# Grouped convolution and per-sample mix: the fp32r parts of x taken straight from the loaded tile, without a tile between

## The chip, the cores and the metric

The kernel runs on one core of a Trainium2 chip. The metric is the device time of one execution in microseconds (us), the median over several runs; smaller is better.

## The reference

The input x has 64 samples of 128 channels by 2048 positions, in fp32. Two residual blocks follow each other:

```python
# L0: grouped convolution along the positions, 4 groups of 32 channels, 9 taps, plus a context per sample
x = x + conv(x, weight, groups=4, padding=4) + (cond @ c_weight.T)[:, :, None] + bias[None, :, None]
# L1: a 128 x 128 matrix per sample, a softmax mixture of 8 matrices
h = gelu(gelu(cond @ W0 + b0) @ W1 + b1)
att = softmax(h @ W2 + b2)
agg_w = einsum('bk,koi->boi', att, weight[..., 0]);  agg_b = att @ bias_k
x = x + einsum('boi,bih->boh', agg_w, x) + agg_b[:, :, None]
```

## The kernel before, in words

The sum is kept near fp32 precision with TensorE's fp32r format: each operand is split into a rounded part (`_hi`) and what the rounding left (`_lo`), and a product is made of three matmuls, hi by hi, hi by lo and lo by hi.

**Phases.** The 2048 positions of a sample are split into PH = 4 phases, position 4n + q being column n of phase q. The convolution of one group of 32 channels is then M = 12 shifted products, 3 matmuls each, so CONV = 36 matmuls of 32 rows by 512 columns. The mix is MIX = 12 matmuls for each phase r. The four groups t run on the four row quarters of TensorE at once, group t LAG = 4 steps behind group t - 1. A slot is the time of one sample: 48 steps of four matmuls. At steps 0 to 35 group 0 convolves sample s, at steps 36 to 47 it mixes sample s - 1; the other groups do the same 4, 8 and 12 steps later.

**Per sample.** SyncE loads x into `x_in` (1 MB, two buffers). ScalarE copies `x_in` to `x_ph`, reading every fourth element (a step of 16 bytes) and writing the four phases one after the other (`split_phases`, L418). VectorE rounds `x_ph` to `x_hi` (`round_x`, a cast, L480) and takes `x_lo` = `x_ph` - `x_hi` (`rest_x`, L486). TensorE convolves into the PSUM tile `y_ps` (L357). ScalarE rounds y to `y_hi` (`round_y`, L428, one for each group), VectorE takes `y_lo` (`rest_y`, L497). GpSimd builds the mix matrix of the sample in `mix_prod`, `mix_sum_f`, `mix_f`, `mix_parts` (`mix_matrix`, L588 to L611); SyncE stores it to DRAM (`store_mix`, L235) and loads it back four times into `mix_rep` (`load_mix`, L247). TensorE mixes (L377), ScalarE takes the sum with the bias to `z_out` (`take_z`, L439, two halves), SyncE stores it (L255).

**Order.** Every engine has its own list, written out by hand. In slot s, SyncE does load_mix(s), store_mix(s + 1), store(s - 2), load(s + AHEAD), with AHEAD = 4; ScalarE does take_z(s - 2) twice, split_phases(s + 2), round_y(s, 0..3); VectorE does round_x(s + 1), rest_x(s + 1), rest_y(s, 0..3). An engine waits at the head of its list, and what stands behind waits too. `x_hi` has two buffers, so that of sample s + 1 can be written when the convolution of sample s - 1 has ended, which is when slot s begins. There is one `y_ps`: group g of the next sample can start when `y_lo` of group g has been taken.

**Start.** VectorE makes the convolution weights (`cw_rep` L501 by a read with a step of 36 bytes, `wt_f`, `wt_lo`, then `cw_lo` L513), then x_hi and x_lo of sample 0. In slot 0 TensorE carries, between its steps, the small matrix products of the softmax, and VectorE the element-wise work of it: att_diag (L541), `rest_x((0, 1))`, then after TensorE's L339 `table` (L545 to L557), on which GpSimd's first mix matrix waits. Samples are counted from 0.

Of the kernel before, what the change touches and what calls it, by code (L numbers as in the profile page):

```python
# [13 lines left out]
U = 4  # L14
Q = 32
DMA = 16
AHEAD = 4
LAG = 4


# [32 lines left out]
def cond_resid_kernel(nc, x, cond, bias, conv_w, ctx_w, w0, b0, w1, b1, w2, b2, mix_w, mix_b, out):  # L53
# [13 lines left out]
    with ExitStack() as stack:  # L67
# [7 lines left out]
            return [make(f"{name}{k}", *args) for k in range(2)]  # L75

        x_in = two(sb, "x_in", [P, T])
        x_ph = two(sb, "x_ph", [P, PH, N])
        x_hi = two(sb, "x_hi", [P, PH, N + 2], F32R)
        x_lo = two(sb, "x_lo", [P, PH, N + 2], F32R)  # L80

# [86 lines left out]
        table_made = sem("table_made")  # L168

        x_loaded = two(sem, "x_loaded")  # L170
        x_split_ph = sem("x_split_ph")

        x_hi_made = sem("x_hi_made")
        x_lo_made = sem("x_lo_made")
# [34 lines left out]
        @block.sync  # L209
        def _(sp):  # L210
            def ahead(*values):

                for v in values:
                    if not isinstance(v, int):
                        sp.compute_val(v)
                return values

            def load(s):
                if not exists(s):
                    return  # L220
                b, taken = ahead(number(s), done(s, lag=-2))

                at_least(sp, x_split_ph, taken)
                sp.dma_start(x_in[buf(s)][:, :], x[b, :, :]).then_inc(x_loaded[buf(s)], DMA)

            def store_mix(s):

                if not exists(s):
                    return
                b = buf(s)  # L230
                made, taken = ahead(done(s), DMA * G * uses(s))
                sp.wait_ge(mix_made, made)

                at_least(sp, mix_loaded[b], taken)
                sp.dma_start(mix_dram[b][:, :, :], mix_parts[b][:, :, :].bitcast(F32)).then_inc(mix_stored[b], DMA)  # L235

            def load_mix(s):

                if not exists(s):
                    return  # L240
                b = buf(s)
                stored, mixed = ahead(DMA * (uses(s) + 1), done(s, PH, lag=-2))
                sp.wait_ge(mix_stored[b], stored)

                at_least(sp, z_ready, mixed)
                for r in range(PH):
                    sp.dma_start(mix_rep[b][Q * r:Q * r + Q, :, :, :].bitcast(F32).rearrange("c g h o -> c g (h o)"),  # L247
                                 mix_dram[b].rearrange("(g c) h o -> c g (h o)", g=G)).then_inc(mix_loaded[b], DMA)

            def store(s):  # L250
                if not exists(s):
                    return
                b, read = ahead(number(s), done(s, 2))
                sp.wait_ge(z_read, read)
                sp.dma_start(out[b, :, :], z_out[buf(s)][:, :]).then_inc(z_stored[buf(s)], DMA)  # L255

            sp.dma_start(cw_nat[:, :, :], conv_w[:, :, :]).then_inc(conv_w_loaded, DMA)
            load((0, 0))
            for to, of in (
                (cond_nat[:, :], cond[:, :]),  # L260
                (ctxw_nat[:, :], ctx_w[:, :]),
                (w0_sb[:, :], w0[:, :]),
                (cols[:, 0:1], bias.rearrange("(c a) -> c a", a=1)),
                (cols[:, 1:2], b0.rearrange("(c a) -> c a", a=1)),
                (cols[:, 2:3], b1.rearrange("(c a) -> c a", a=1)),
                (mixb_sb[:, :], mix_b[:, :]),
                (w1_sb[:, :], w1[:, :]),
                (w2_sb[:, :], w2[:, :]),
                (b2_sb[:, :], b2.rearrange("(a k) -> a k", a=1)),
                (mixw_nat[:, :, :], mix_w.rearrange("k o i a -> o k (i a)")),  # L270
            ):
                sp.dma_start(to, of).then_inc(weights_loaded, DMA)
            load((0, 1))
            load((0, 2))
            load((0, 3))

            store_mix((0, 0))

            def slot(s):
                load_mix(s)  # L280
                store_mix(after(s, 1))
                store(after(s, -2))
                load(after(s, AHEAD))

            pipeline(sp, slot)
            sp.wait_ge(z_stored[0], DMA * (NS // 2))
            sp.wait_ge(z_stored[1], DMA * (NS // 2))
# [121 lines left out]

        @block.scalar  # L410
        def _(act):
            def split_phases(s):
                if not exists(s):
                    return
                act.wait_ge(x_loaded[buf(s)], DMA * (uses(s) + 1))

                at_least(act, x_lo_made, done(s, lag=-2))
                nc.scalar.activation(x_ph[buf(s)][:, :, :], x_in[buf(s)][:, :].rearrange("c (n q) -> c q n", q=PH),  # L418
                                     ACT.Copy).then_inc(x_split_ph, 1)

            def round_y(s, g):
                if not exists(s):
                    return
                act.wait_ge(y_ready, done(s, G, lag=-1) + g + 1)

                if g == 0:
                    at_least(act, z_ready, done(s, PH, lag=-2))
                nc.scalar.activation(y_hi[buf(s)][:, g, :], y_ps[:, g, :], ACT.Copy).then_inc(y_hi_made, 1)  # L428

            def take_z(s, h):  # L430
                if not exists(s):
                    return
                act.wait_ge(z_ready, done(s, PH, lag=-1) + 2 * h + 2)
                if h == 0:
                    act.wait_ge(par_made, done(s))

                    at_least(act, z_stored[buf(s)], DMA * uses(s))
                pair = slice(2 * h, 2 * h + 2)
                nc.scalar.activation(z_out[buf(s)][:, :].rearrange("c (n q) -> c n q", q=PH)[:, :, pair],  # L439
                                     z_ps[:, pair, :].rearrange("c q n -> c n q"),  # L440
                                     ACT.Identity, bias=par[s[1]][:, NK:NK + 1]).then_inc(z_read, 1)

            def copy(o, i):
                return nc.scalar.activation(o, i, ACT.Copy)

            split_phases((0, 0))
            copy_taps(act, (2, 3), copy)
            act.wait_ge(wt_split, 1)
            act.wait_ge(cw_cleared, 1)
            for r in range(PH):  # L450
                copy(cw_hi[:, r:r + K, Q * r:Q * r + Q], wt_hi[:, :, :].bitcast(F32)).then_inc(cw_hi_placed, 1)
            split_phases((0, 1))

            act.wait_ge(weights_loaded, DMA * 11)
            act.wait_ge(mlp_mm, 1)
            nc.scalar.activation(h1[:, :], ps[:, 5, 0:NS], ACT.Gelu, bias=cols[:, 1:2]).then_inc(mlp_act, 1)
            act.wait_ge(mlp_mm, 2)
            nc.scalar.activation(h2[:, :], ps[:, 5, 0:NS], ACT.Gelu, bias=cols[:, 2:3]).then_inc(mlp_act, 1)
            act.wait_ge(soft, 3)
            nc.scalar.activation(expd[:, :], logit[:, :], ACT.Exp, bias=ntop[:, 0:1]).then_inc(mlp_act, 1)  # L460

            def slot(s):
                take_z(after(s, -2), 0)
                take_z(after(s, -2), 1)
                split_phases(after(s, 2))

                for g in range(G):
                    round_y(s, g)

            pipeline(act, slot)  # L470

        @block.vector
        def _(dve):
            def round_x(s):
                if not exists(s):
                    return
                dve.wait_ge(x_split_ph, done(s))

                at_least(dve, y_ready, done(s, G, lag=-2))
                nc.vector.tensor_copy(x_inner(x_hi[buf(s)]), x_ph[buf(s)][:, :, :]).then_inc(x_hi_made, 1)  # L480

            def rest_x(s):
                if not exists(s):
                    return
                dve.wait_ge(x_hi_made, done(s))
                nc.vector.tensor_tensor(x_inner(x_lo[buf(s)]), x_ph[buf(s)][:, :, :],  # L486
                                        x_inner(x_hi[buf(s)]).bitcast(F32), ALU.subtract).then_inc(x_lo_made, 1)

            def rest_y(s, g):
# [22 lines left out]
            for r in range(PH):  # L512
                nc.vector.tensor_copy(cw_lo[:, r:r + K, Q * r:Q * r + Q], wt_lo[:, :, :].bitcast(F32)  # L513
                                      ).then_inc(cw_lo_placed, 1)
            round_x((0, 0))
            rest_x((0, 0))

            dve.wait_ge(cond_turned, 1)
            nc.vector.tensor_copy(cond_t[:, :], ps[:, 4, 0:NS]).then_inc(cond_copied, 1)
            nc.vector.tensor_copy(ctxw_t[:, :], ps[:, 4, P:2 * P]).then_inc(cond_copied, 1)  # L520
            nc.vector.tensor_copy(mixb_t[:, :], ps[:, 4, 3 * P:3 * P + NK]).then_inc(cond_copied, 1)
            round_x((0, 1))
            dve.wait_ge(ctx_mm, 1)
            nc.vector.tensor_scalar(ctx_c[:, :], ps[:, 4, 0:NS], cols[:, 0:1], None, ALU.add).then_inc(ctx_made, 1)
            dve.wait_ge(mixw_turned, 1)
# [33 lines left out]

            def slot(s):  # L560
                if not is_sample(s, 0):
                    round_x(after(s, 1))
                    rest_x(after(s, 1))
                for g in range(G):
                    rest_y(s, g)
# [76 lines left out]
```

## Time and profile before

| what | value |
|---|---|
| time, median of 3 runs | 765.26 us (765.18 to 767.09) |
| the profiled execution | 765.69 us, its span 763.9 us |
| TensorE (PE) busy | 739.5 us, 97% of the span |
| VectorE (DVE), ScalarE (ACT), GpSimd (POOL) busy | 413.8, 557.0, 440.6 us |
| mean granted TensorE clock | 0.983 of full speed |

The span runs from the first to the last instruction; the 1.8 us between the span and the profiled execution's own time lie around it. Four matmuls overlap on TensorE, so its busy time is the time in which at least one ran, not the sum of their durations.

### The profile page before, as it was taken

Reading aid. Unit: us, or ns where it says so; the run is one execution under the profiler, and the core shown is the slowest. Engines: PE = TensorE matmul, PEld = TensorE weight load, DVE = VectorE, ACT = ScalarE, POOL = GpSimd, SP = SyncE. Lnnn points to the kernel's source line nnn. Section 1 sums busy time; section 2 is a strip of 40 time slices with the busy share of each in tenths; the row PEclk is TensorE's granted clock in tenths of the full one; section 3 lists DMA queues with packets and bytes.
Section 4 is the critical chain, followed back from the end, with each engine's and each line's share of the span. In section 5 each row is a group of like instructions: output and inputs, shape, how many; then the busy total and the mean of one; then the engine's idle time right before and its main releaser. Section 6 shows DMA issues by size and latency. Waiting matters only on the chain.

```text
span 763.9 us, 29144 instructions
## 1 busy us (share of the span) xinstructions
PE 739.5 (97%) x12347; PEld 702.7 (92%) x12347; DVE 413.8 (54%) x410; ACT 557.0 (73%) x460; POOL 440.6 (58%) x589
## 2 busy tenths in 40 slices
PE   3969999999999999999999999999999999999997
PEld 2749999999999999999999999999999999999996
DVE  4355666456555655654565556456555645654541
ACT  5426787777777777777777787787788777777843
POOL 1079997665565566556556655655665565556510
PEclk8789999999999999999999999999999999999999
DMA  6116987766676676667667766766776676677534
GB/s 222 46 35 188 296 292 264 275 240 233 248 277 238 224 271 239 239 242 281 239 224 265 252 237 235 284 236 226 259 263 234 233 280 239 227 255 266 189 120 179
DMA packets 66824, 177.43 MB, mean 232 GB/s; under 512 B 7850, under 2 KB 50418, under 8 KB 50418
## 3 DMA queue, kind: packets, MB, share of 16 engines
q1 hardware_dynamic: 66802, 177.10, 65.6%
q8 instruction: 18, 0.29, 0.2%
q14 instruction: 4, 0.03, 0.0%
HBM read 101.57 MB, written 75.50 MB: 232 GB/s over the span
## 4 chain that ended last, share of the span: by engine, by line
PE 95%; DMA 1%; POOL 1%; DVE 1%; ACT 1%; issue 0%; SPq 0%
PE ps L357 76%; PE ps L377 18%; DMA x_in<-in_x_dram 1%; POOL mix_prod L598 1%; ACT x_ph L418 0%; DMA mix_rep<-mix_dram 0%; DVE x_lo L486 0%; POOL mix_prod L593 0%; PE ps L333 0%; DMA mix_dram<-mix_parts 0%; PE ps L316 0%; DVE cw_lo L513 0%; SPq L247 0%; ACT z_out L439 0%; DVE x_hi L480 0%
## 5 line engine op out<-in xcount | busy, mean ns | idle before, releaser
L357 PE MATMUL ps<-x_hi,cw_hi 32*128 32x512 f32 x3072 | 648.2, 392 | 10.1 <-DVE x_lo L486 7.4
L357 PE MATMUL ps<-x_lo,cw_hi 32*128 32x512 f32 x3072 | 648.0, 392 | 0.0
L357 PE MATMUL ps<-x_hi,cw_lo 32*128 32x512 f32 x3072 | 647.7, 392 | 0.0
L357 PEld LDWEIGHTS ps<-x_hi,cw_hi 32*128 32x128 f32 x3072 | 498.6, 185 | 17.4 <-issue 10.7
L357 PEld LDWEIGHTS ps<-x_lo,cw_hi 32*128 32x128 f32 x3072 | 499.4, 185 | 6.7 <-issue 0.8
L357 PEld LDWEIGHTS ps<-x_hi,cw_lo 32*128 32x128 f32 x3072 | 500.1, 185 | 5.6 <-issue 0.6
L497 DVE TENSOR_TENSOR y_lo<-ps,y_hi 128x512 fp32r<-128x512 f32 x256 | 177.0, 692 | 312.8 <-ACT y_hi L428 311.8
L377 PE MATMUL ps<-y_hi,mix_rep 32*128 32x512 f32 x2048 | 337.9, 387 | 3.5 <-DMA mix_rep<-mix_dram 3.5
L377 PE MATMUL ps<-y_lo,mix_rep 32*128 32x512 f32 x1024 | 285.8, 386 | 0.0
L377 PEld LDWEIGHTS ps<-y_hi,mix_rep 32*128 32x128 f32 x2048 | 254.7, 184 | 12.8 <-DMA mix_rep<-mix_dram 3.9
L418 ACT ACTIVATE x_ph<-x_in 128x2048 f32<-128x2048 f32 x64 | 250.2, 3910 | 4.6 <-DMA x_in<-in_x_dram 4.6
L428 ACT ACTIVATE y_hi<-ps 128x512 fp32r<-128x512 f32 x256 | 153.4, 599 | 121.4 <-PE ps L357 121.4
L439 ACT ACTIVATE z_out<-ps,par 128x1024 f32<-128x1024 f32 x128 | 153.6, 1200 | 62.9 <-PE ps L377 62.9
L377 PEld LDWEIGHTS ps<-y_lo,mix_rep 32*128 32x128 f32 x1024 | 188.0, 184 | 4.5
L588 POOL COPY par<-table 128x9 f32 (+1 forms) x64 | 41.0, 641 | 257.2 <-ACT z_out L439 217.1
L486 DVE TENSOR_TENSOR x_lo<-x_ph,x_hi 128x2048 fp32r<-128x2048 f32 x64 | 149.5, 2336 | 2.2
L598 POOL TENSOR_TENSOR mix_prod<-mix_prod 128x512 f32<-128x512 f32 (+1 forms) x128 | 136.5, 1066 | 10.0
L593 POOL TENSOR_TENSOR mix_prod<-mixw_t,par 128x512 f32<-128x512 f32 x128 | 132.7, 1058 | 5.2
L480 DVE CAST x_hi<-x_ph 128x2048 fp32r<-128x2048 f32 x64 | 79.9, 1249 | 0.1
L605 POOL TENSOR_TENSOR mix_f<-mix_sum_f,ident 128x128 f32<-128x128 f32 x64 | 32.5, 507 | 5.0
L601 POOL TENSOR_TENSOR mix_sum_f<-mix_prod 128x128 f32<-128x128 f32 x64 | 32.5, 507 | 5.0
L611 POOL TENSOR_TENSOR mix_parts<-mix_f,mix_parts 128x128 fp32r<-128x128 f32 x64 | 31.6, 494 | 5.0
(68 smaller groups left out, 80.6 us busy)
## 6 DMA issues: line engine op xcount, KB each, us to landing
x_in<-in_x_dram SPq DMA_DIRECT2D x64, 1024.0 KB, 4.9
out_dram<-z_out SPq DMA_DIRECT2D x64, 1024.0 KB, 4.2
mix_rep<-mix_dram SPq DMA_DIRECT2D x256, 128.0 KB, 2.5
mix_dram<-mix_parts SPq DMA_DIRECT2D x64, 128.0 KB, 2.2
mixw_nat<-in_L_cond_weight_dram SPq DMA_DIRECT2D x1, 512.0 KB
cw_nat<-in_L_cond_weight_dram SPq DMA_DIRECT2D x1, 144.0 KB, 2.2
w_sb<-in_L_cond_W_dram SPq DMA_DIRECT2D x2, 64.0 KB
ctxw_nat<-in_L_cond_c_weight_dram SPq DMA_DIRECT2D x1, 64.0 KB
```

Of the source, the lines that this page charges most:

```text
L357: mm = pe.matmul(y_ps[:, g, :], w[rows, m, :], x_at(xx[buf(s)], rows, m), start=i == 0, stop=i == CONV - 1)
L377: mm = pe.matmul(z_ps[:, r, :], mix_rep[buf(s)][rows, g, h, :], yy[buf(s)][rows, g, :], start=i == 0, stop=i == MIX - 1)
L418: nc.scalar.activation(x_ph[buf(s)][:, :, :], x_in[buf(s)][:, :].rearrange("c (n q) -> c q n", q=PH), ACT.Copy).then_inc(x_split_ph, 1)
L428: nc.scalar.activation(y_hi[buf(s)][:, g, :], y_ps[:, g, :], ACT.Copy).then_inc(y_hi_made, 1)
L439: nc.scalar.activation(z_out[buf(s)][:, :].rearrange("c (n q) -> c n q", q=PH)[:, :, pair], z_ps[:, pair, :].rearrange("c q n -> c n q"), ...
L480: nc.vector.tensor_copy(x_inner(x_hi[buf(s)]), x_ph[buf(s)][:, :, :]).then_inc(x_hi_made, 1)
L486: nc.vector.tensor_tensor(x_inner(x_lo[buf(s)]), x_ph[buf(s)][:, :, :], x_inner(x_hi[buf(s)]).bitcast(F32), ALU.subtract).then_inc(x_lo_ma ...
L497: nc.vector.tensor_tensor(y_lo[buf(s)][:, g, :], y_ps[:, g, :], y_hi[buf(s)][:, g, :].bitcast(F32), ALU.subtract).then_inc(y_lo_made, 1)
L588: nc.gpsimd.tensor_copy(par[s[1]][:, :], table[:, number(s), :]).then_inc(par_made, 1)
L593: nc.gpsimd.tensor_tensor(mix_prod[:, ks, :], mixw_t[:, ks, :], par[s[1]][:, ks].unsqueeze(2).broadcast_to([P, NK // 2, P]), ALU.mult).the ...
L598: nc.gpsimd.tensor_tensor(mix_prod[:, 0:half, :], mix_prod[:, 0:half, :], mix_prod[:, half:2 * half, :], ALU.add).then_inc(mix_sum, 1)
L601: nc.gpsimd.tensor_tensor(mix_sum_f[:, :], mix_prod[:, 0, :], mix_prod[:, 1, :], ALU.add).then_inc(mix_sum, 1)
```

## The change

ScalarE's copy writes `x_hi` directly, in fp32r, from `x_in` (it is now called `round_x`), and VectorE's subtraction reads `x_in` with a step of four elements, 16 bytes, in place of `x_ph`. The tile `x_ph`, its semaphore and VectorE's cast go. `round_x` stands first in ScalarE's slot, for sample s + 1 in place of s + 2, and has the wait on `y_ready` that the cast had. A buffer of `x_in` is now free only when `x_lo` has been made; AHEAD goes from 4 to 3, and the load of sample 3 moves from the start of SyncE's list into slot 0, behind load_mix and store_mix.

```diff
-AHEAD = 4
+AHEAD = 3
...
-        x_ph = two(sb, "x_ph", [P, PH, N])
...
-                at_least(sp, x_split_ph, taken)
+                at_least(sp, x_lo_made, taken)
                 sp.dma_start(x_in[buf(s)][:, :], x[b, :, :]).then_inc(x_loaded[buf(s)], DMA)
...
             load((0, 1))
             load((0, 2))
-            load((0, 3))
...
-            def split_phases(s):
+            def round_x(s):
+
                 if not exists(s):
                     return
                 act.wait_ge(x_loaded[buf(s)], DMA * (uses(s) + 1))
 
-                at_least(act, x_lo_made, done(s, lag=-2))
-                nc.scalar.activation(x_ph[buf(s)][:, :, :], x_in[buf(s)][:, :].rearrange("c (n q) -> c q n", q=PH),
-                                     ACT.Copy).then_inc(x_split_ph, 1)
+                at_least(act, y_ready, done(s, G, lag=-2))
+                nc.scalar.activation(x_inner(x_hi[buf(s)]), x_in[buf(s)][:, :].rearrange("c (n q) -> c q n", q=PH),
+                                     ACT.Copy).then_inc(x_hi_made, 1)
...
-            split_phases((0, 0))
+            round_x((0, 0))
...
-            split_phases((0, 1))
+            round_x((0, 1))
...
             def slot(s):
+                if not is_sample(s, 0):
+                    round_x(after(s, 1))
                 take_z(after(s, -2), 0)
                 take_z(after(s, -2), 1)
-                split_phases(after(s, 2))
...
-            def round_x(s):
-                if not exists(s):
-                    return
-                dve.wait_ge(x_split_ph, done(s))
-
-                at_least(dve, y_ready, done(s, G, lag=-2))
-                nc.vector.tensor_copy(x_inner(x_hi[buf(s)]), x_ph[buf(s)][:, :, :]).then_inc(x_hi_made, 1)
-
             def rest_x(s):
                 if not exists(s):
                     return
                 dve.wait_ge(x_hi_made, done(s))
-                nc.vector.tensor_tensor(x_inner(x_lo[buf(s)]), x_ph[buf(s)][:, :, :],
+                nc.vector.tensor_tensor(x_inner(x_lo[buf(s)]), x_in[buf(s)][:, :].rearrange("c (n q) -> c q n", q=PH),
                                         x_inner(x_hi[buf(s)]).bitcast(F32), ALU.subtract).then_inc(x_lo_made, 1)
...
-            round_x((0, 0))
             rest_x((0, 0))
...
-            round_x((0, 1))
...
             def slot(s):
                 if not is_sample(s, 0):
-                    round_x(after(s, 1))
                     rest_x(after(s, 1))
                 for g in range(G):
                     rest_y(s, g)
```

## Rows read from the trace of the kernel before

**Rows 1.** The page: the chain that ended last, share of the span by engine.

```profile
PE 95%; DMA 1%; POOL 1%; DVE 1%; ACT 1%; issue 0%; SPq 0%
```

**Rows 2.** Busy time by window: stretch, its length, each engine, clock, DMA, GB/s.

```profile
409.10:420.20 11.10, 11.10 (x196) 10.68 (x193) 6.19 (x6) 8.61 (x7) 6.55 (x9) 1.00 0.68 248
```

**Rows 3.** Groups by shape: busy us, mean ns of one, idle before and its releaser.

```profile
L418 ACT ACTIVATE x_ph<-x_in 128x2048 f32<-128x2048 f32 x64 | 250.2, 3910 | 4.6 <-DMA x_in<-in_x_dram 4.6
...
L497 DVE TENSOR_TENSOR y_lo<-ps,y_hi 128x512 fp32r<-128x512 f32 x256 | 177.0, 692 | 312.8 <-ACT y_hi L428 311.8
L439 ACT ACTIVATE z_out<-ps,par 128x1024 f32<-128x1024 f32 x128 | 153.6, 1200 | 62.9 <-PE ps L377 62.9
...
L486 DVE TENSOR_TENSOR x_lo<-x_ph,x_hi 128x2048 fp32r<-128x2048 f32 x64 | 149.5, 2336 | 2.2
...
L598 POOL TENSOR_TENSOR mix_prod<-mix_prod 128x512 f32<-128x512 f32 x64 | 84.6, 1323 | 5.0
...
L501 DVE COPY cw_rep<-cw_nat 128x1152 f32<-128x1152 f32 x1 | 2.2, 2216 | 3.0 <-DMA cw_nat<-in_L_cond_weight_dram 3.0
```

**Rows 4.** Timeline of the start: start us, length us, what, idle before.

```profile
6.64 3.84 ACT L418 ACTIVATE x_ph<-x_in 128x2048 f32<-128x2048 f32 x1 [4.61 <-DMA x_in<-in_x_dram]
...
12.21 1.53 DVE L513 CAST cw_lo<-wt_lo 128x288 fp32r<-128x288 f32 x4
...
14.91 2.29 DVE L486 TENSOR_TENSOR x_lo<-x_ph,x_hi 128x2048 fp32r<-128x2048 f32 x1
...
17.34 0.76 PE L357 MATMUL ps<-x_hi,cw_hi 32*128 32x512 f32 x1 [7.40 <-DVE x_lo L486]
```

**Rows 5.** Timeline of VectorE and ScalarE from the end of slot 0.

```profile
34.31 2.28 DVE L486 TENSOR_TENSOR x_lo<-x_ph,x_hi 128x2048 fp32r<-128x2048 f32 x1
39.30 0.69 DVE L545 COPY table<-ps 128x512 f32<-128x512 f32 x1 [2.71 <-PE ps L339]
...
44.61 1.22 DVE L480 CAST x_hi<-x_ph 128x2048 fp32r<-128x2048 f32 x1
45.86 3.25 DVE L486 TENSOR_TENSOR x_lo<-x_ph,x_hi 128x2048 fp32r<-128x2048 f32 x1
...
40.91 3.94 ACT L418 ACTIVATE x_ph<-x_in 128x2048 f32<-128x2048 f32 x1
```

**Rows 6.** The chain that ended last, in slot 1: start us, us, what.

```profile
44.81 2.16 POOL mix_prod L598
...
47.04 2.68 POOL mix_prod L598
```

**Rows 7.** Timeline of TensorE in slot 1, and one window behind the stall.

```profile
57.50 0.49 PE L377 MATMUL ps<-y_hi,mix_rep 32*128 32x512 f32 x1 [3.51 <-DMA mix_rep<-mix_dram]
...
59.00:60.00 1.00, 1.00 (x16) 0.84 (x12) 0.52 (x1) 0.45 (x1) 1.00 (x2) 0.50 0.39 129
```

**Rows 8.** SyncE's load in slot 0, landings (its own; first nine), y_hi ending slots 1, 2.

```profile
58.70 1.11 SPq L224 DMA_DIRECT2D x_in<-in_x_dram  x1
...
x_in<-in_x_dram SPq DMA_DIRECT2D x1, 1024.0 KB, 6.0
...
DMA to landing us min/median/max: 4.8/6.2/9.5
...
62.19 0.60 ACT L428 ACTIVATE y_hi<-ps 128x512 fp32r<-128x512 f32 x1 [1.02 <-PE ps L357]
...
73.30 0.60 ACT L428 ACTIVATE y_hi<-ps 128x512 fp32r<-128x512 f32 x1 [0.33 <-PE ps L357]
```

**Rows 9.** Timeline of ScalarE, VectorE and GpSimd in one steady slot.

```profile
406.60 0.60 ACT L428 ACTIVATE y_hi<-ps 128x512 fp32r<-128x512 f32 x1 [0.33 <-PE ps L357]
...
417.72 0.60 ACT L428 ACTIVATE y_hi<-ps 128x512 fp32r<-128x512 f32 x1 [0.33 <-PE ps L357]
...
415.57 0.69 DVE L497 TENSOR_TENSOR y_lo<-ps,y_hi 128x512 fp32r<-128x512 f32 x1 [4.18 <-ACT y_hi L428]
...
410.79 0.65 POOL L588 COPY par<-table 128x9 f32 x1 [4.03 <-ACT z_out L439]
```

More of the change, by code:

```diff
@@ L170, in cond_resid_kernel @@
         x_loaded = two(sem, "x_loaded")
-        x_split_ph = sem("x_split_ph")
         x_hi_made = sem("x_hi_made")
```

## Prediction

> **What bounds the kernel now.** The page comes first. TensorE is busy for 97% of the span (the table above), and the chain that ended last lies on it for 95% [rows 1]. So the steady part can only get longer, if one of the other engines comes late, and a gain has to come from the 5% in which the chain is elsewhere. The view of windows says the same of one steady slot: TensorE 11.10 us of 11.10, VectorE 6.19, ScalarE 8.61, GpSimd 6.55 [rows 2]. Two ends of a convolution lie 417.72 - 406.60 = 11.12 us apart [rows 9]; that is the slot.
>
> The timeline of the start then shows what is not TensorE's: it waits until 17.34 for x_lo of sample 0 [rows 4]. Later it stands 3.51 us until 57.50 for the first mix matrix [rows 7]. The chain leads back from there through GpSimd's additions [rows 6], the softmax table on VectorE at 39.30 [rows 5] and TensorE's own slot 0 to that start at 17.34. It is one serial path: what is added to x_lo of sample 0 or to GpSimd's first matrix moves everything behind it.
>
> **The price of the new read.** No row shows a subtraction with one input at a step of 16 bytes. The nearest ones are L501, a VectorE copy reading at 36 bytes, 2216 ns for 1152 elements, and L418, the ScalarE copy that already reads `x_in` at 16 bytes, 3910 ns for 2048. The contiguous x_lo takes 2.28 us for 2048 elements when nothing disturbs it [rows 5], y_lo 0.69 for 512 [rows 3]: (2280 - 692) / 1536 = 1.03 ns an element and some 0.15 us fixed. Then L501 is (2216 - 150) / 1152 = 1.79 ns an element. L418 is 1.91 ns, or 1.83 with 0.15 us fixed too; y_hi on the same engine, 512 elements out of PSUM in 0.60 us [rows 9], is under 1.2 even with its fixed part. Two engines come to the same 1.8 ns, so I take it for the stepped read itself: x_lo = 2048 x 1.80 + 150 = 3.83 us, 1.55 more than now. Bounds: 2.28 if the second input's stream hides the step; 2048 x (1.80 + 1.03) + 150 = 5.95 if the stepped input adds its whole time to the other's. I take 3.83, since the contiguous subtraction reads two inputs in 1.03 ns an element and so shows no turns taken, and the two stepped rows agree.
>
> The Trainium skill (SBUF — State Buffer, section "Specifications (TRN2)") says that SBUF has lines of 16 bytes and needs two hits in a line for full bandwidth; at this step each line is hit once. It gives no price, so by the page the sum is only more than with 2.28; the trace's L501 and L418 agree.
>
> ScalarE's copy keeps its input pattern and its 2048 elements; only the output's type and place change. y_hi is written in that type at 0.60 us for 512 [rows 9]. I keep 3.91 us.
>
> **Steady slots.** Let the convolution of a sample end at 406.60 [rows 9]. ScalarE does the last y_hi (0.60), then round_x to 411.1, then the two z_out (1.20 each) to 413.5. Its next y_hi is due at about 414.9 (y_lo at 415.57 follows it by some 0.65), so ScalarE has 1.4 us to spare. VectorE, which waited there 4.18 us [rows 9], makes x_lo from 411.1 to 414.9 and is free for that y_lo at 415.57. TensorE wants x_lo and y_lo at 417.72; x_lo has 2.8 us to spare, 0.7 less with y_lo behind it. A wait for a GpSimd instruction (below, at most 1.32) still fits. The two z_out end 2.7 us later than now (GpSimd's par followed them at 410.79), and GpSimd, which idled 4.03 us for them, starts at 413.5; TensorE wants them only at step 36, 8.3 us into the slot, and they are there at 6.9. So the 60 steady slots cost nothing. Without these covers each us would cost 60.
>
> **The shared resource.** In slot 1 VectorE's cast and x_lo (44.61 to 49.11, [rows 5]) meet GpSimd's two additions, 2.16 and 2.68 us [rows 6], where the larger one has a mean of 1.32 [rows 3]; x_lo takes 3.25 in place of 2.28. The times fit turns taken by whole instructions: the first addition ends about 1.1 after the cast ends at 45.83, x_lo ends 2.2 after that, the second addition 0.6 after x_lo. So a longer x_lo holds GpSimd longer. Per slot GpSimd's 6.55 and x_lo's 3.83 are 10.4 of 11.12, against 6.55 + 1.22 + 2.28 = 10.05 now: it still fits.
>
> **Start.** VectorE ends cw_lo at 13.7; cast and x_lo followed, to 14.91 + 2.29 = 17.20 [rows 4]. ScalarE's x_hi is there from 6.64 + 3.84 = 10.5, so x_lo runs from 13.65 to 17.48. The cast's 1.25 (from 13.65 to 14.91) is won, 1.55 is lost: **+0.3**. x_lo of sample 1 starts at 34.31 and grows by 1.55 into the 2.71 us that VectorE waits before the table [rows 5]: nothing, but beyond 4.9 us it would be paid. The cast of sample 1 taken away there stood before a wait for TensorE: nothing won.
>
> **First mix matrix.** ScalarE's copy for sample 2 runs from 40.91 to 44.85 [rows 5], the place where the split for sample 3 was. GpSimd's first addition starts at 44.81, just ahead, to 46.13; x_lo follows to 49.96; the second addition ends 0.6 later at 50.57, where it was 49.72: **+0.85**. If x_lo gets in first it is 44.85 + 3.83 + 1.32 + 0.8 = 50.8, +1.1; with 2.28 it is 49.0, -0.7. The matrix is what TensorE stands for, so this counts in full.
>
> **Samples 3 and 4.** The load of sample 3 now stands in SyncE's slot 0 behind load_mix(0) and store_mix(1), which wait for GpSimd; it goes out where the load of sample 4 did, 58.70, and lands 6.0 later, 64.7 [rows 8]. ScalarE would be ready at 62.8. So x_hi of sample 3 is 64.7 to 68.6; z_out, queued behind, is at 69.8 and 71.0, just before steps 36 and 44 (62.2 + 8.3 = 70.5, and 72.4). x_lo is 68.7 to 72.5, or to 73.8 behind one GpSimd addition, then the first y_lo 0.69 behind it: 73.2 to 74.5. Slot 3 wants both at 73.30 [rows 8]. Between 0 and 1.2; GpSimd, freed of the cast and x_lo that now come later, is then in the middle of the next matrix, so I take **+0.7**. The following loads have SyncE's order behind GpSimd too, but their wait is for slots that begin 11 us later each, and they land in time by about 1 us.
>
> Sum: 0.3 + 0.85 + 0.7 = +1.85 on the profiled execution's 765.69, 767.5. That execution is 0.43 above the median of the runs, so 767.1 against 765.26. The end of the kernel (last mix, z_out, store) has none of the changed work.
>
> **The rivals.** *The step costs VectorE nothing* (x_lo 2.28): -1.25 at the start, -0.7 at the first matrix, no stall at slot 3: -1.95, 763.3. For it: a second stream could cover the latency. Against: L501 and L418. A variant: the stepped subtraction no longer takes turns with GpSimd; then the additions shrink from 4.9 to 2.1 us, and with +0.3 it is -2.5, 762.8. Against it: nothing says that the step changes the ports. I give the two 0.15, of which 0.09 ends over 0.3% faster.
>
> *One load less ahead bites.* If the load of sample 3 lands after 9.5 us (the first nine took 4.8 to 9.5 [rows 8]) in place of 6.0, x_lo is 3.5 later, TensorE stands 4.2 us at slot 3, and the sum is +5.35, 770.6. It may lose clock too: after the 3.51 us stall the granted clock was 0.50, the 1.2 GHz level, between 59 and 60 [rows 7]; if that lasts 3 us it costs 1.5 more, 772.1. It decides from a landing of about 6.5 us on; each us beyond costs one. Against: the load goes out at the very place of the one that took 6.0. 0.18.
>
> *The two inputs are read in turn* (5.95): GpSimd and x_lo need 6.55 + 5.95 = 12.5 us of a slot of 11.12, 1.4 x 60 = 84 us more, 850. It decides from x_lo of 4.5 us on. Against: both nearest rows lie well under. 0.03. The Trainium skill (SBUF — State Buffer, section "SBUF: two separate sides") has the port pair that VectorE and GpSimd share as a lock held for a whole instruction, also by a VectorE instruction with two SBUF inputs against a GpSimd one that reads SBUF. By it all of x_lo's length counts, as in this rival and in the +0.85; the trace's 2.16 and 2.68 us agree.
>
> **How the numbers follow.** The forecast has 0.57, of its own range 765.5 to 768.3; a measurement of this kernel can tell about 0.3%, 2.3 us, from no change, and of the forecast 0.12 lies above that. With the rivals, and 0.07 for what I have not seen (0.04 of it faster): faster 0.13, same 0.54, slower 0.33. The range 763.2 to 770.0 leaves out the variant that stops taking turns, the reads in turn and the worse half of the late load.
>
> **What would show it.** After: x_lo at 3.8 us mean 3.83 with one form; no cast; TensorE's first matmul at 17.6; the stall for mix_rep 0.9 longer; a wait of under 1.2 us for x_lo or y_lo near 75; 11.1 us slots from then on. Wrong if x_lo is under 3 or over 4.5 us, if ScalarE waits for x_in beyond sample 3, or if TensorE waits in the steady slots.

## The result, and the profile after

The changed kernel takes 767.33 us, the median of 20 runs (765.85 to 771.25), beside 765.38 (764.42 to 768.25) for the kernel before. The ratio is 1.0023 with a 95% interval of 1.0012 to 1.0034: slower by 1.8 us, between 0.9 and 2.6. The forecast was 767.1, with 765.5 to 768.3 as its own range, so the time came out as forecast. The profiled execution took 766.97 us, its span 765.1 us, 1.2 more than the span before.

The page's busy times after:

```profile
PE 739.8 (97%) x12347; PEld 727.8 (95%) x12347; DVE 435.7 (57%) x346; ACT 540.2 (71%) x460; POOL 492.0 (64%) x589
...
PE 95%; POOL 1%; DMA 1%; DVE 1%; ACT 1%; issue 0%; SPq 0%
...
L477 DVE TENSOR_TENSOR x_lo<-x_in,x_hi 128x2048 fp32r<-128x2048 f32 x64 | 247.6, 3868 | 191.0 <-ACT x_hi L416 191.0
...
L416 ACT ACTIVATE x_hi<-x_in 128x2048 fp32r<-128x2048 f32 x64 | 249.3, 3895 | 6.6 <-DMA x_in<-in_x_dram 6.6
```

The chain is still TensorE's for 95% [rows 1]. VectorE has 64 instructions less (the casts) and is busy 22 us longer: x_lo has a mean of 3.87 us where it had 2.34 [rows 3]. ScalarE's copy is where it was, 3.90.

The windows view of a steady slot, to be held against [rows 2]:

```profile
409.10:420.20 11.10, 11.10 (x200) 11.10 (x196) 6.61 (x6) 8.32 (x8) 7.42 (x10) 1.00 0.71 253
```

TensorE fills it as before. GpSimd's 7.42 is 0.9 more than before; that is not work, as its own timeline shows for that stretch:

```profile
414.64 1.53 POOL L576 COPY par<-table 128x9 f32 x1 [3.21 <-ACT z_out L437]
416.25 2.04 POOL L581 TENSOR_TENSOR mix_prod<-mixw_t,par 128x512 f32<-128x512 f32 x2
```

The copy of nine columns, which takes 0.19 us when VectorE is doing something else (0.65 in the same place before, [rows 9]), takes 1.53 behind x_lo. GpSimd still idles 3.21 us before it, so nobody waits.

Where the 1.2 us of the span arose is read from ScalarE, VectorE and TensorE at marks that both traces have. After, timeline:

```profile
13.30 3.80 DVE L477 TENSOR_TENSOR x_lo<-x_in,x_hi 128x2048 fp32r<-128x2048 f32 x1
...
17.25 0.76 PE L354 MATMUL ps<-x_hi,cw_hi 32*128 32x512 f32 x1 [8.04 <-DVE x_lo L477]
...
39.67 0.69 DVE L534 COPY table<-ps 128x512 f32<-128x512 f32 x1 [1.13 <-PE ps L336]
...
58.45 0.49 PE L374 MATMUL ps<-y_hi,mix_rep 32*128 32x512 f32 x1 [3.78 <-DMA mix_rep<-mix_dram]
...
74.23 0.60 ACT L426 ACTIVATE y_hi<-ps 128x512 fp32r<-128x512 f32 x1 [0.32 <-PE ps L354]
...
85.69 0.60 ACT L426 ACTIVATE y_hi<-ps 128x512 fp32r<-128x512 f32 x1 [0.31 <-PE ps L354]
...
418.99 0.60 ACT L426 ACTIVATE y_hi<-ps 128x512 fp32r<-128x512 f32 x1 [0.32 <-PE ps L354]
```

The last y_hi of slot 3 in the kernel before, which no group of rows above has:

```profile
84.42 0.60 ACT L428 ACTIVATE y_hi<-ps 128x512 fp32r<-128x512 f32 x1 [0.33 <-PE ps L357]
```

| mark | before | after | later by | this part |
|---|---|---|---|---|
| the table on VectorE begins | 39.30 [rows 5] | 39.67 | 0.37 | start 0.37 |
| TensorE gets the first mix matrix | 57.50 [rows 7] | 58.45 | 0.95 | first matrix 0.58 |
| last y_hi of slot 2 | 73.30 [rows 8] | 74.23 | 0.93 | |
| last y_hi of slot 3 | 84.42 | 85.69 | 1.27 | slot 3 0.34 |
| last y_hi, slot 33 | 417.72 [rows 9] | 418.99 | 1.27 | 30 slots: 0.00 |

Three small losses at the start, and nothing from then on. The second is read from these rows, VectorE's x_lo of sample 2 and GpSimd's two additions, which took 4.90 us before:

```profile
45.26 4.84 DVE L477 TENSOR_TENSOR x_lo<-x_in,x_hi 128x2048 fp32r<-128x2048 f32 x1 [0.20 <-ACT x_hi L416]
...
45.18 5.47 POOL L586 TENSOR_TENSOR mix_prod<-mix_prod 128x512 f32<-128x512 f32 x2
```

The third is read from the load of sample 3 and what follows it:

```profile
59.64 1.28 SPq L222 DMA_DIRECT2D x_in<-in_x_dram  x1
...
65.69 3.90 ACT L416 ACTIVATE x_hi<-x_in 128x2048 fp32r<-128x2048 f32 x1 [1.95 <-DMA x_in<-in_x_dram]
...
69.61 3.85 DVE L477 TENSOR_TENSOR x_lo<-x_in,x_hi 128x2048 fp32r<-128x2048 f32 x1 [5.16 <-ACT x_hi L416]
73.38 2.47 DVE L488 TENSOR_TENSOR y_lo<-ps,y_hi 128x512 fp32r<-128x512 f32 x4
```

ScalarE stood 1.95 us for that load. VectorE was then so late with x_lo that the first y_lo of sample 2, whose y_hi had been there since 72.2, began at 73.38, and slot 3 cannot begin without it.

### The profile page after: what moved, and what is told of

Read it like the earlier page. It is cut to its first block, busy times and chain, and to the rows that moved or that the text cites. A ratio compares the mean times of both kernels' runs of the same rounds, so it can differ in the third digit from the quotient of the medians.

```text
span 765.1 us, 29046 instructions
## 1 busy us (share of the span) xinstructions
PE 739.8 (97%) x12347; PEld 727.8 (95%) x12347; DVE 435.7 (57%) x346; ACT 540.2 (71%) x460; POOL 492.0 (64%) x589
## 4 chain that ended last, share of the span: by engine, by line
PE 95%; POOL 1%; DMA 1%; DVE 1%; ACT 1%; issue 0%; SPq 0%
PE ps L354 74%; PE ps L374 19%; POOL mix_prod L586 1%; DMA x_in<-in_x_dram 1%; DVE x_lo L477 0%; ACT x_hi L416 0%; DMA mix_rep<-mix_dram 0%; POOL mix_prod L581 0%; PE ps L330 0%; PE ps L313 0%; DMA mix_dram<-mix_parts 0%; DVE cw_lo L504 0%; SPq L245 0%; ACT z_out L437 0%; PE ps L336 0%
## 5 line engine op out<-in xcount | busy, mean ns | idle before, releaser
L354 PE MATMUL ps<-x_lo,cw_hi 32*128 32x512 f32 x3072 | 656.2, 393 | 0.0
L354 PEld LDWEIGHTS ps<-x_hi,cw_hi 32*128 32x128 f32 x3072 | 477.3, 185 | 13.2 <-issue 11.7
L354 PEld LDWEIGHTS ps<-x_lo,cw_hi 32*128 32x128 f32 x3072 | 478.1, 185 | 2.5 <-issue 0.8
L354 PEld LDWEIGHTS ps<-x_hi,cw_lo 32*128 32x128 f32 x3072 | 477.9, 185 | 2.0 <-issue 0.6
L477 DVE TENSOR_TENSOR x_lo<-x_in,x_hi 128x2048 fp32r<-128x2048 f32 x64 | 247.6, 3868 | 191.0 <-ACT x_hi L416 191.0
L374 PEld LDWEIGHTS ps<-y_hi,mix_rep 32*128 32x128 f32 x2048 | 267.0, 184 | 5.0 <-DMA mix_rep<-mix_dram 4.2
L416 ACT ACTIVATE x_hi<-x_in 128x2048 fp32r<-128x2048 f32 x64 | 249.3, 3895 | 6.6 <-DMA x_in<-in_x_dram 6.6
L576 POOL COPY par<-table 128x9 f32 (+1 forms) x64 | 87.3, 1364 | 210.6 <-ACT z_out L437 170.2
L437 ACT ACTIVATE z_out<-ps,par 128x1024 f32<-128x1024 f32 x128 | 143.4, 1181 | 4.3 <-PE ps L374 4.3
L596 POOL TENSOR_TENSOR mix_parts<-mix_sum_f,ident 128x128 fp32r<-128x128 f32 x64 | 33.3, 520 | 0.0
```

The costliest lines, as they stand in the source:

```text
L354: mm = pe.matmul(y_ps[:, g, :], w[rows, m, :], x_at(xx[buf(s)], rows, m), start=i == 0, stop=i == CONV - 1)
L374: mm = pe.matmul(z_ps[:, r, :], mix_rep[buf(s)][rows, g, h, :], yy[buf(s)][rows, g, :], start=i == 0, stop=i == MIX - 1)
L416: nc.scalar.activation(x_inner(x_hi[buf(s)]), x_in[buf(s)][:, :].rearrange("c (n q) -> c q n", q=PH), ACT.Copy).then_inc(x_hi_made, 1)
L477: nc.vector.tensor_tensor(x_inner(x_lo[buf(s)]), x_in[buf(s)][:, :].rearrange("c (n q) -> c q n", q=PH), x_inner(x_hi[buf(s)]).bitcast(F32 ...
L576: nc.gpsimd.tensor_copy(par[s[1]][:, :], table[:, number(s), :]).then_inc(par_made, 1)
L596: nc.gpsimd.tensor_tensor(mix_parts[buf(s)][:, 0, :], mix_sum_f[:, :], ident[:, :], ALU.add).then_inc(mix_hi_made, 1)
```

## The experiments

### x_lo read contiguously: what the step alone costs

VectorE's input is read without a step; x_lo then holds other numbers, all else is equal.

```diff
-x_in[buf(s)][:, :].rearrange("c (n q) -> c q n", q=PH)
+x_in[buf(s)][:, :].rearrange("c (q n) -> c q n", q=PH)
```

> The changed kernel, but VectorE's subtraction reads x_in contiguously (so x_lo holds other numbers; same count of elements, same waits). Theory 1 (the step's price counts at three places): x_lo 2.28 us; against the changed kernel the start is 1.55 us earlier, the first mix matrix 1.5 us, and the 0.3 us gap at slot 3 goes, 3.4 us in all, some 764 us. Theory 2 (the order, one sample ahead, and the later load cost the time, not the step): x_lo is shorter but the time stays near 767.3. Steady slots 11.1 us under both.

Measured: 763.88 us, ratio to the kernel before 0.9979 (0.9968 to 0.9990). Against the changed kernel's 1.0023 that is 0.0044, or 3.4 us. Timeline of VectorE and GpSimd:

```profile
13.31 2.28 DVE L477 TENSOR_TENSOR x_lo<-x_in,x_hi 128x2048 fp32r<-128x2048 f32 x1
...
37.90 0.69 DVE L534 COPY table<-ps 128x512 f32<-128x512 f32 x1 [2.71 <-PE ps L336]
...
43.40 4.02 POOL L586 TENSOR_TENSOR mix_prod<-mix_prod 128x512 f32<-128x512 f32 x2
```

From the same 13.3, the table comes at 37.90 in place of 39.67: 1.8 for 1.5 that x_lo is shorter. The pair of additions takes 4.02 in place of 5.47, and TensorE gets the first mix matrix at 55.17, another 1.5 earlier; the gap at slot 3 gives the last 0.3. Theory 1 holds, and theory 2 falls: without the step, the same order and the same later load are 1.6 us **faster** than the kernel before. The change is a gain (a cast less at the start, and a shorter collision) that the step of 16 bytes eats up and more.

That the three places add up so well is partly luck, because two effects outside theory 1 cancel. Behind the shorter stall the granted clock stayed at 1.00 from 58 to 64, where it was 0.72 in the mean in both kernels, which is worth about 1.6 us. And ScalarE stood 3.77 us for the load of sample 3, z_out came late behind it, and TensorE waited 1.22 us for that.

### Other steps: 8 bytes, 32 bytes, and both inputs at 16

Each is the changed kernel with another access pattern in the subtraction (x_lo holds other numbers). The input patterns alone, for 8 bytes, for 32 bytes, and for both inputs at 16 bytes:

```diff
+                                        x_in[buf(s)][:, :].rearrange("c (h n q) -> c h q n", h=2, q=2)[:, :, :, 0:N],
...
+                                        x_in[buf(s)][:, :].rearrange("c (n q h) -> c q h n", q=PH, h=2),
...
+                                        x_in[buf(s)][:, :].rearrange("c (p n q) -> c p q n", p=PH, q=4),
+                                        x_inner(x_hi[buf(s)]).bitcast(F32).rearrange("c p (n q) -> c p q n", q=4),
```

> The changed kernel, but VectorE's subtraction reads x_in with a step of 8 bytes (x_lo holds other numbers). If a 16-byte line that is hit twice is read at full rate: x_lo 2.28 us. If every step but one element costs: 3.85 us, or something between.

> The changed kernel, but VectorE's subtraction reads x_in with a step of 32 bytes (x_lo holds other numbers). If what counts is only that each element lies in another 16-byte line: 3.85 us as at 16 bytes. If the price grows with the step: more, up to double.

> The changed kernel, but VectorE's subtraction reads x_in and x_hi both with a step of 16 bytes (x_lo holds other numbers). If the two inputs are read side by side, the slower sets the pace: 3.85 us. If the second stepped input adds its own 0.8 ns an element: 5.5 us, and then GpSimd and VectorE need more than a slot and the kernel gets tens of us slower.

The view of x_lo's line, one row of each of the three, in this order (shortest, median and longest in ns):

```profile
L477 DVE TENSOR_TENSOR x_lo<-x_in,x_hi x64: 2276/2293/3352, 13.8 to 733.1; 128x2048 fp32r<-128x2048 f32 x64
```

```profile
L477 DVE TENSOR_TENSOR x_lo<-x_in,x_hi x64: 3901/4270/5057, 13.3 to 735.4; 128x2048 fp32r<-128x2048 f32 x64
```

```profile
L477 DVE TENSOR_TENSOR x_lo<-x_in,x_hi x64: 3783/3870/4911, 13.6 to 734.4; 128x2048 fp32r<-128x2048 f32 x64
```

Measured times, one run each: 765.57, 767.85 and 766.93 us. They can't be ordered: the run at 8 bytes is 2.3 us above the profiled run of the contiguous read with the same x_lo. The durations of x_lo can.

At 8 bytes there is no price at all, 2.29 us. At 16 it is 3.85. Twice the step adds some 10% in the median, 4.27, but the undisturbed first one took 3.90, hardly more than the 3.80 at 16 bytes; what lengthens the others was not traced. And a second input at 16 bytes adds nothing, 3.87. The forecast's upper bound of 5.95, in which one stepped input adds its whole time to the other's, is excluded by the 3.85 itself. The row of the Trainium skill on SBUF's 16-byte lines (SBUF — State Buffer, section "Specifications (TRN2)") agrees with this case: two hits in a line, 2.29; one, 3.85; that 32 bytes cost a little more than 16 it does not say. No step between 8 and 16 bytes was tried.

### x_lo of sample 2 held back: the collision on the path

```diff
                 dve.wait_ge(x_hi_made, done(s))
+                if is_sample(s, 2):
+                    dve.wait_ge(mix_made, 1)
```

> The changed kernel; VectorE also waits for the first mix matrix (mix_made 1) before x_lo of sample 2, so that the two don't meet. Theory 1 (x_lo and GpSimd's additions take turns by whole instructions and the matrix of sample 0 is on the path): the two additions take 2.1 us in place of 5.5, TensorE's stall for mix_rep falls from 3.8 to 0.5 us. But x_lo of sample 2 then meets the second matrix, SyncE's load of sample 3 stands behind that one's store and goes out at about 59.5 again, lands at 65.5, and slot 2 now begins at about 58 to 60: x_lo of sample 3 comes 3 to 4 us late and most of the gain is given back, 765 to 767. Rival (the additions are slow for another reason): the pair stays at over 5 us and nothing moves, 767.3.

Measured: 767.75 us, ratio to before 1.0033 (1.0020 to 1.0046). GpSimd's timeline, where the pair of 5.47 us (45.18 to 50.65 in the changed kernel) is gone and now a later pair is long, and the copy of sample 3 on ScalarE:

```profile
44.58 2.08 POOL L588 TENSOR_TENSOR mix_prod<-mix_prod 128x512 f32<-128x512 f32 x2
...
49.01 5.48 POOL L583 TENSOR_TENSOR mix_prod<-mixw_t,par 128x512 f32<-128x512 f32 x2
...
64.83 3.87 ACT L416 ACTIVATE x_hi<-x_in 128x2048 fp32r<-128x2048 f32 x1 [6.34 <-DMA x_in<-in_x_dram]
```

The waits of TensorE have no mix_rep row any more; in its place stands this one:

```profile
PE ps L374 <- ACT z_out L437: 3.7, 1, 3.7
```

The windows view of slot 2's end (the changed kernel had a granted clock of 1.00 there):

```profile
70.00:81.00 11.00, 11.00 (x153) 10.01 (x157) 6.68 (x6) 8.29 (x8) 10.09 (x11) 0.79 0.61 195
```

The collision is as theory 1 stated, and its rival falls. TensorE no longer stands for the matrix, so slot 2 begins 5.3 us earlier (last y_hi of slot 1 at 57.88 in place of 63.13), but the load of sample 3 goes out at 59.14, only 0.5 us earlier. What gives the gain back is that late load, but by another path than expected. x_lo was in time, before slot 2 ended. It is ScalarE that waits 6.34 us for the load at the head of its list, z_out stands behind, and TensorE waits 3.7 us for that. The expectation was 765 to 767; the rest is clock. During that stall the granted clock fell to 0.50 and stayed there from 68 to 74.5, while the changed kernel was at 0.50 only from about 59.5 to 62.5; against it slot 2 lost 2.5 us beyond the stall and slot 1 won 0.9, 1.6 us on balance. This is the forecast's rival "one load less ahead bites", brought about.

### The same with the load earlier

In both, `load(after(s, AHEAD))` is moved to the head of SyncE's slot; the first has the hold too.

> As hold, and in SyncE's slot load(s + 3) stands first, ahead of load_mix and store_mix. Theory 1: the load of sample 3 goes out when x_lo of sample 1 is made (39 us), ScalarE waits for no x_in after sample 1, nothing is given back: 3.3 us for the stall, up to 1.6 for the clock that does not fall behind it, 0.3 for the gap at slot 3 against the changed kernel, 762 to 764. Rival (load order does not matter): equal to hold.

> The changed kernel with SyncE's load(s + 3) first in the slot, nothing else. Theory 1 (the 0.3 us gap at slot 3 comes from the late load of sample 3): no wait of ScalarE for x_in of sample 3, no gap at slot 3, y_hi of group 3 of two samples 11.1 us apart from slot 2 on. Rival (the gap comes from something else): the gap stays.

Measured: 765.03 us (ratio 1.0003, 0.9991 to 1.0015) with the hold, and 770.82 without it (one run). The first misses its 762 to 764; for the second no time was forecast. SyncE's timeline of the second, and TensorE's wait in it:

```profile
53.32 0.33 SPq L233 DMA_DIRECT2D mix_dram<-mix_parts  x1
53.69 0.43 SPq L222 DMA_DIRECT2D x_in<-in_x_dram  x1
55.02 1.76 SPq L245 DMA_DIRECT2D mix_rep<-mix_dram  x4
```

```profile
PE ps L374 <- DMA mix_rep<-mix_dram: 6.9, 1, 6.9
```

My edit was wrong, not the theory's mechanism: the first slot's load still stands behind store_mix(0) in the list, so the 1 MB went out at 53.69, right in front of the four loads of mix_rep that TensorE stands for, and the stall grew from 3.78 to 6.9 us (3.0 with the hold). In both, ScalarE waits for no x_in after sample 1, as theory 1 had it, and the gap at slot 3 is gone. The rival of the first, "load order does not matter", falls: 765.03 against 767.75. A load is late in one place and in the way in another.

### The load of sample 3 back at its old place

```diff
             load((0, 2))
+            load((0, 3))
...
-                load(after(s, AHEAD))
+                if not is_sample(s, 0):
+                    load(after(s, AHEAD))
```

> The changed kernel with one edit: the load of sample 3 is put back before store_mix(0), and skipped in slot 0. Theory 1 (the gap at slot 3 comes from that load's lateness): x_lo of sample 3 ends some 2 us before slot 3 begins, no gap there, the two ends of the convolutions of samples 2 and 3 are 11.1 us apart in place of 11.46. Rival: the gap stays, then it is from y_lo of sample 2 or from z_out.

Measured: 766.61 us (one run, which alone can't tell 0.3 us). The trace can. The last y_hi of slots 2 and 3 on ScalarE:

```profile
74.18 0.60 ACT L428 ACTIVATE y_hi<-ps 128x512 fp32r<-128x512 f32 x1 [0.34 <-PE ps L356]
...
85.30 0.60 ACT L428 ACTIVATE y_hi<-ps 128x512 fp32r<-128x512 f32 x1 [0.34 <-PE ps L356]
```

They are 11.12 us apart; in the changed kernel it was 11.46 (85.69 - 74.23). By this trace the third loss is the load's.

### Half of x_lo once more: when turns taken become the bound

VectorE makes phases 0 and 1 of x_lo first, waits for them, then makes all four.

> The changed kernel; VectorE first makes phases 0 and 1 of x_lo, then all four: 2.0 + 3.85 us a sample, 5.9 in all with the gap. Theory 1 (x_lo and GpSimd's instructions take turns, so their sum must fit into a slot): 6.6 + 5.9 = 12.5 us against 11.1, GpSimd falls behind by 1.3 us a slot and after some ten slots sets the pace, slots of 12.4, 50 to 85 us slower in all. Rival (only VectorE's own time counts, 5.9 + 2.8 of 11.1, and its x_lo is due 6.6 us after x_hi): under 15 us slower, GpSimd waits little.

Measured: 811.01 us (one run), 44 more than the changed kernel. The waits, and the windows view of a steady stretch:

```profile
PE ps L355 <- DVE y_lo L494: 22.1, 54, 3.4
...
POOL par L582 <- POOL mix_parts L605: 17.1, 57, 0.6
```

```profile
400.00:412.40 12.40, 12.20 (x212) 10.79 (x208) 9.10 (x6) 9.05 (x8) 11.37 (x10) 1.00 0.71 233
```

VectorE and GpSimd in one slot:

```profile
414.12 2.86 DVE L478 TENSOR_TENSOR x_lo<-x_in,x_hi 128x1024 fp32r<-128x1024 f32 x1 [2.56 <-ACT x_hi L417]
417.01 4.16 DVE L483 TENSOR_TENSOR x_lo<-x_in,x_hi 128x2048 fp32r<-128x2048 f32 x1
...
417.61 3.84 POOL L595 TENSOR_TENSOR mix_sum_f<-mix_prod 128x128 f32<-128x128 f32 x1
```

The rival falls, since it allowed under 15 us: by VectorE's own time it would fit (from the last y_hi 4.4 us to x_hi, 5.9 and 0.6, 10.9 of 11.1). Theory 1 has the mechanism but the size is off. Slots are 11.64 us (last y_hi at 409.67 and 421.31), not 12.4, and TensorE waits for y_lo, 54 times. GpSimd waits for no other engine's result any more, only for its own mix_parts and for its turns: it sets the pace. The first part of x_lo takes 2.86 in place of 1.99 because a GpSimd instruction is running, and GpSimd's mix_sum_f takes 3.84 in place of 0.46. GpSimd's chain for one sample with the gaps between its instructions, about 6.7, and the two parts of x_lo, 5.8, are 12.5 us and share 11.64: 0.9 of it overlaps. At each change of turn the instruction that had to wait ends sooner behind the other than its own length: the second addition at 417.53, 0.55 behind x_lo's first part (alone it takes 0.8), and mix_sum_f at 421.45, 0.28 behind the whole x_lo (alone 0.46).

### All three cures, on both kernels

The hold on sample 2; the load that used to collide put before store_mix(0) in SyncE's list; the other loads first in their slots.

> The changed kernel with three edits: VectorE holds x_lo of sample 2 until mix_made 1; the load of sample 3 stands in SyncE's list before store_mix(0), so that it can't run into the loads of mix_rep; from slot 1 on load(s + 3) stands first. Theory 1 (what held the two kernels with the hold back was the late load, or the load in front of mix_rep): additions 2.1 us, stall for mix_rep under 0.8 us, no wait of ScalarE for x_in of sample 3, 762 to 763.8. Rival (the stall for mix_rep comes back in another form): 765 or more, as hold_loadfirst.

> The kernel before with the same three edits (here the load of sample 4 moves before store_mix(0)). Theory 1: no wait of ScalarE for x_in, 761 to 762.5; it stays some 0.3 to 1 us under the changed kernel with the same edits, since of the change's three costs only the one at the start is left. Rival (the change helps once the collisions are gone, by the cast that is missing): the changed one is at or under this one.

Measured: the changed kernel 764.57 us, ratio to before 0.9989 (0.9978 to 1.0001); the kernel before 763.40 us, 0.9972 (0.9962 to 0.9982). The hold alone on the kernel before:

> The kernel before; VectorE also waits for the first mix matrix before the cast and x_lo of sample 2. Theory 1: GpSimd's two additions 2.1 us in place of 4.9, the stall for mix_rep from 3.5 to 0.7 us, 2.8 us faster and up to 1.6 more for the clock, less some 0.6 for ScalarE's copy of sample 4, which gets its data late: 761.5 to 764 against 765.4. It tells whether the kernel before, given the same cure, keeps its lead over the changed one.

gave 764.04 us, 0.9975 (0.9961 to 0.9989), so the loads add nothing clear there. TensorE's waits in the changed kernel with all three:

```profile
PE ps L356 <- DVE x_lo L481: 7.5, 1, 7.5
...
PE ps L356 <- DVE y_lo L492: 2.7, 1, 2.7
PE ps L376 <- DMA mix_rep<-mix_dram: 1.6, 2, 0.9
```

TensorE no longer waits for the first matrix, and x_in is there in time, but both medians are about 1 us above what was expected. The two waits for mix_rep are for later matrices. In slot 1 the load of x goes out at 58.84 and the loads of mix_rep behind it at 60.19, and TensorE stands 0.92 us for them, until 66.83. In slot 4 it stands 0.66 us, until 89.99, again for loads of mix_rep issued behind one of x:

```profile
78.92 0.77 SPq L253 DMA_DIRECT2D out_dram<-z_out  x1
79.74 0.43 SPq L222 DMA_DIRECT2D x_in<-in_x_dram  x1
80.51 2.88 SPq L245 DMA_DIRECT2D mix_rep<-mix_dram  x4
```

So the rival "the stall comes back in another form" is right in part. The profiled execution took 763.33 us, inside the expected 762 to 763.8; what the median has above it, 1.2 us, no trace shows.

The fastest versions of the study are those of the kernel **before**, with the hold alone or with all three edits: the change does not pay even where its collisions are cured. Its rival ("the missing cast helps once the collisions are gone") falls: the intervals of the two ratios just overlap, but in 105 of the 120 pairs of their 12 and 10 runs the changed kernel is the slower one.

## Why the prediction was right

**The price of the read**: 3.83 us from L501 and L418, measured 3.80 at the start and 3.85 in the median. 2.28 is what 8 bytes or no step cost, and the two inputs do not add. How closely the number hit is partly luck: L501 reads at 36 bytes, and the subtraction at 32 bytes took 4.27 in the median, so VectorE does not have one price for every step beyond 16.

**Steady slots**: no cost, as forecast; 0.00 over 30 slots. GpSimd's start moved by 2.6 us against the convolution, where 2.7 was worked out. That its first copy would then end only with x_lo (1.53 us in place of 0.65) was not worked out; the slack covered it.

**Start, +0.3**: x_lo takes from 13.30 to 17.10, 3.80, where cast and x_lo took 3.55: +0.25. The mark shows +0.37, and this agreement is luck: TensorE's first matmul came at 17.25, 0.09 earlier than before and not at the 17.6 forecast, and the table was late all the same. In this execution the data of sample 0 came 0.4 us earlier (ScalarE's first copy starts at 6.24 in place of 6.64), and the granted clock reached 1.00 about 1 us later (0.62 between 28 and 29, where it was 0.65 between 27 and 28), which costs about 0.5 at half the clock. So the mark is 0.25 - 0.35 + 0.46. The contiguous read, from the same 13.3, is the cleaner evidence.

**First matrix, +0.85**: measured 0.58. The order of turns was right (the first addition ahead, x_lo, the second addition). The term was too large because an instruction that waits for its turn overlaps the end of the other: x_lo ended 4.92 us after the first addition began, not 5.15, and the second addition 0.56 behind it (0.61 before).

**Samples 3 and 4, +0.7**: measured 0.34, and load3 shows that it is the load. It landed after 6.0 us, as the row promised. VectorE did not have to wait for a GpSimd instruction here (x_lo from 69.61 took 3.85), which was the upper half of my span of 0 to 1.2 and my reason for 0.7.

Sum 1.27 in the trace, 1.76 (0.9 to 2.6) from the ratio of the runs, 1.85 forecast. The mechanism at each place held, and two of the three terms were too large, by 0.27 and 0.36. That the runs lie nearer to the forecast than the trace is luck of the executions: the profiled one of the kernel before took 0.31 more than its median of 20, the one after 0.36 less.

**The rivals**: that the step costs nothing is excluded; that the late load costs more did not happen here, and hold shows how near it was. It also shows that this rival had the wrong path: it let TensorE stand at slot 3 for x_lo, but a later load first delays z_out, which the forecast itself had at 69.8, only 0.7 before step 36. That the two inputs are read in turn is excluded by the 3.85 and by both16; its threshold of 4.5 us was too strict, since at 5.8 us of x_lo slots were 11.64 us and not 12.5.

## What to carry to other kernels

An edit that removes a pass over the data can move its strided read to an engine that had read contiguously; look for the row of that engine, or of any, at that step, and price it at every place where the instruction lies on the start's chain. Where the steady part is full on one engine and the others keep their slack (5.8 us of x_lo no longer did), an edit elsewhere changes only the first few samples, so follow these one by one, transfers included. Before a load is moved, list what is issued behind it: in this study the same 1 MB load was late in one place and in the way in another.

## What the runs showed of the hardware

- VectorE's two-input subtraction: 1.03 ns an element contiguous and at 8 bytes, 1.8 at 16 bytes, about 2.0 at 32 in the median (4.27 us; the first one 3.90), and the same 1.8 with both inputs at 16 bytes.
- GpSimd's instructions and VectorE's subtraction of two SBUF tiles take turns by whole instructions, with a small overlap: an instruction of GpSimd that had to wait ended 0.55 to 0.6 us after the subtraction where alone it takes 0.8, 0.28 after it where alone it takes 0.46, and the copy of 0.19 ended together with it. Sums of the two engines' times are therefore somewhat too high as a bound (12.5 against 11.64).
- The moment at which TensorE's granted clock rises after the start moved by 1 us between two profiled executions whose first convolution began within 0.1 us of each other, worth about 0.5 us.
- Not every low clock is in the record: in before_hold and hold_loadfirst the granted clock reads 1.00 between 17 and 28, but the matmuls near 20 took 0.62 us each, as in the kernel before at 0.50. Their higher mean clock, 0.993, is no sign of a faster execution.
